# A state-space stage's time-step products at the first chunk, its decay mask on VectorE and its row gate on GpSimd

## The chip, the cores and the metric

The kernel runs on one core of one Trainium2 chip. The metric is the time of one execution on the device in microseconds (us), lower is better; where several runs are shown, their median counts.

## The reference, cut to what matters

The program is a whole eight-layer hybrid model over 8 sequences of 512 rows and 256 features. The change lies in the seventh layer alone, the state-space layer (512 inner features in 8 heads of 64, a state of 128):

```python
zxbcdt = u @ W_in
z, xBC, dt = split(zxbcdt)            # 512, 768 and 8 columns
dt = softplus(dt + dt_bias)
A = -exp(A_log)
xBC = silu(causal_conv_4(xBC, conv_w) + conv_b)
x, Bm, Cm = split(xBC)                # 512, 128, 128
y = ssd(x * dt, A * dt, Bm, Cm)       # decays exp(segsum), masked to the past
y = y.reshape(b, l, D_INNER)
y = (y - mu) * rsqrt(var + 1e-05) * norm_w
y = y * silu(z)
return y @ W_out
```

## The kernel before, in words

The stage is `state_space_stage`. It goes over the 8 sequences (the code calls each a batch, b) and cuts each into four chunks of 128 rows (c). Each engine has its own program, written out by hand and kept in step with the others by counting semaphores; nothing is reordered by a scheduler. The order of the work is the order of these four programs:

- `front` fills the pipeline with the projections of batch 0. Then `back(b, ...)` runs once per batch, and on TensorE it also carries the projections of batch b + 1 (`project`, 6 of them for the columns that are convolved and 4 for z), placed between the chunks of batch b. The last batch has none to carry.
- TensorE per chunk: `chunk_inputs` (L2196) transposes x, B and spreads the cumulative decays (`psX`, `psG`, `psC`), L2235 multiplies by the state, L2241 makes the state's update, and L2247 multiplies by the masked decays `lt` (result in `psY`).
- ScalarE turns `psC` into decays: `decays` (L2346) makes `lt` of 8 heads x 128 with Relu and Exp.
- GpSimd per chunk, in this order: `xdec` (L2414), which TensorE's L2241 needs; `st2` (L2418), which VectorE's state update needs; and the mask, `lt` times `gm` (L2422), which TensorE's L2247 needs.
- VectorE per chunk: `state` (L2514), `output` (L2522 adds up y; L2528 and L2530 take its statistics; L2532 is the gate, (y - mean) * silu(z)), `chunk_inputs(c + 2)` (L2496, L2501, L2502), `output_from_state` (L2507) and one `convolve` of the next batch (L2436, three operations).
- After the four chunks TensorE transposes the gated rows (L2255), multiplies them by the output weights (L2276, into the first 256 columns of `psG`), and VectorE adds the result to X (L2558). Between the first two transposes stands `project_dt` (L2154), the time-step products of batch b + 1: 24 products with 8 columns each, for the high and low halves of rows and weights, into `psO`. VectorE takes them with `dt_biased` (L2440) after the last chunk; `dt_decay`, `sum_dt` and `dt_sums` follow in the output part.

Of the kernel before, what the change touches and what calls it, by code (L numbers as in the profile page):

```python
# [2011 lines left out]
class StateSpaceWeights:  # L2012
# [3 lines left out]
    def __init__(self, core, w_in, conv_w, conv_b, dt_bias, a_log, norm_w, w_out, upto):  # L2016
# [3 lines left out]
        self.win_hi, self.win_lo = core.halves("sw_win_hi", [P, KD, WIN]), core.halves("sw_win_lo", [P, KD, WIN])  # L2020
        self.wout = sb("sw_wout", [P, KI, D])
# [7 lines left out]
        self.win_hi_done, self.win_done = core.sem("sw_win_hi_done"), core.sem("sw_win_done")  # L2029
        self.sources = (w_in, conv_w, conv_b, dt_bias, a_log, norm_w, w_out, upto)  # L2030
# [17 lines left out]
    def vector(self, nc, dve, b):  # L2048

        k = b - 3  # L2050
        if k in range(KD):
            dve.wait_ge(self.win_hi_done, k + 1)
            nc.vector.tensor_tensor(self.win_lo[:, k, :], self.win[:, k, :], self.win_hi[:, k, :],
                                    ALU.subtract).then_inc(self.win_done, 1)


def state_space_stage(nc, core, tag, sw):
# [5 lines left out]
    with ExitStack() as ctx:  # L2063
# [25 lines left out]
        psX = core.psum(f"{tag}_psX", [P, 512], ctx)  # L2089
        psG = core.psum(f"{tag}_psG", [P, 512], ctx)  # L2090
        psC = core.psum(f"{tag}_psC", [P, 2, 512], ctx)
# [12 lines left out]
            sem("yo_ps"), sem("yd_ps"), sem("st_ps"), sem("yo_done"), sem("y_done"), sem("st_done"), sem("st_step"))  # L2104
        ybn_done, ymv_done, yroot_done, yr_done, yz_done = (
# [13 lines left out]
        def _(pe):  # L2119
# [34 lines left out]
            def project_dt(b):  # L2154

                for j in range(TPB):
                    rows, out = slice(j * P, (j + 1) * P), psO[:, j * HM:(j + 1) * HM]
                    for k in range(KD):
                        dt_hi, dt_lo = win_hi[:, k, WIN - HM:WIN], win_lo[:, k, WIN - HM:WIN]
                        nc.tensor.matmul(out, x_hi[:, k, rows], dt_hi, start=(k == 0), stop=False)  # L2160
                        nc.tensor.matmul(out, x_hi[:, k, rows], dt_lo, start=False, stop=False)
                        last = nc.tensor.matmul(out, x_lo[:, k, rows], dt_hi, start=False, stop=(k == KD - 1))
                last.then_inc(dt_ps, 1)

            def sum_dt(b, v):

                steps = dv2[:, v, A].rearrange("p c h -> p (c h)")
                pe.wait_ge(dt_step, b * 7 + 4)
# [4 lines left out]
            def front():  # L2173
# [3 lines left out]
                pe.wait_ge(sw.win_done, KD)  # L2177
                for p in range(2):
# [8 lines left out]
            def back(b, u, more):  # L2187
# [6 lines left out]
                pe.wait_ge(dt_step, at(7, 7))  # L2194

                def chunk_inputs(c):  # L2196
# [25 lines left out]
                for c in range(TPB):  # L2222
# [13 lines left out]
                    if more and c:  # L2236
                        project(b + 1, 1 - u, 2 + c)
                    if c + 1 < TPB:
# [3 lines left out]
                                         start=True, stop=True).then_inc(st_ps, 1)  # L2242
                    pe.wait_ge(m_done, at(TPB, c + 1))
# [15 lines left out]
                if more:  # L2259
                    pe.wait_ge(yo_done, at(TPB - 1, TPB - 1))  # L2260
                    project_dt(b + 1)
                turn_gated(1)
                for j in range(TPB):
                    if j >= 2:
                        turn_gated(j)
                    if more:
                        project(b + 1, 1 - u, NCT + j)
                        if j == 2:
                            sum_dt(b + 1, 1 - u)
# [13 lines left out]
        def _(act):  # L2283
# [28 lines left out]
            def softplus(b, v):  # L2312

                dv = dv2[:, v]
                act.wait_ge(dt_step, b * 7 + 1)
# [22 lines left out]
            def back(b, u, more):  # L2338
# [4 lines left out]
                act.wait_ge(dt_step, at(7, 7))  # L2343
# [55 lines left out]
        def _(pool):  # L2399
# [4 lines left out]
            for b in range(B):  # L2404
                at = lambda per, c: b * per + c
                dv = dv2[:, b % 2]
                for c in range(TPB):
# [12 lines left out]
                    pool.wait_ge(lexp_done, at(TPB, c + 1))  # L2420
                    pool.wait_ge(g_done, at(TPB, c + 1))
                    tt(lt[:, c % 2], lt[:, c % 2], spread(gm[:, c % 2, :], [P, HM, P], 1), ALU.mult).then_inc(m_done, 1)  # L2422

        @block.vector
        def _(dve):
# [14 lines left out]
            def dt_biased(b, v):  # L2440
                dv = dv2[:, v]
                dve.wait_ge(dt_ps, b + 1)
                raw = psO[:, 0:TPB * HM].rearrange("p (c h) -> p c h", h=HM)
# [1182 lines left out]
```

## Time and profile before

| | before |
| --- | --- |
| median of 3 runs | 2611.42 us (2602.41 to 2615.07) |
| the profiled execution: its time, its span | 2603.77 us, 2601.8 us |
| mean granted TensorE clock | 0.957 of full speed |
| busy share of the span: PE, DVE, ACT, POOL | 86%, 68%, 54%, 44% |
| the state-space stage | 2091 to 2521 us of the span |
| first L2247 of a batch in the middle of the stage, and of the next | 2183.43, 2234.62 us |

PE is TensorE, DVE VectorE, ACT ScalarE, POOL GpSimd. The shares are means over stages with quite different limits, so the stage has to be read by itself. The granted clock is a share of full speed: 1.00 is 2.4 GHz, 0.50 is 1.2 GHz. The ends of matmuls are modelled, so neighbouring ones overlap in the rows, and starts are the safer figures.

### The profile page before, as it was taken

The numbers are of one execution on the slowest core, as the hardware profiler recorded it, in microseconds if no ns is written. First come the engines' busy times: TensorE is split into PE (matmuls) and PEld (weight loads), VectorE is DVE, ScalarE is ACT, GpSimd is POOL, SyncE is SP. The second block draws the span as 40 slices with busy tenths as digits, with TensorE's granted clock in tenths as the row PEclk, the third lists the DMA queues.
The fourth block names the chain that finished last, engine by engine and source line by source line (L and its number), as shares of the span: only waits on it lengthen the run. The fifth ranks groups of instructions, "written<-read, shape, count | busy, mean of one in ns | idle before, by whom it ended". The sixth has DMA issues, their size and how long they took to land. (4 is left out here: it accounts for less than half of the span.)

```text
span 2601.8 us, 56542 instructions
## 1 busy us (share of the span) xinstructions
PE 2230.6 (86%) x20944; PEld 1661.6 (64%) x20944; DVE 1773.7 (68%) x4400; ACT 1394.8 (54%) x2127; POOL 1155.8 (44%) x1181
## 2 busy tenths in 40 slices
PE   7957767777899898989899887999797979999979
PEld 4535555556797555555455455898566957777768
DVE  6666778777667667767767764896453558778753
ACT  4631222223342388878888885556111467777753
POOL 4438999992101267657656753000563012233220
PEclk9979999999899899999999999999999989999999
DMA  5454444551100111111111110000000000000001
GB/s 175 146 162 151 143 136 144 160 163 50 58 1 26 44 59 62 58 53 58 50 48 61 61 55 17 20 1 2 14 1 27 13 0 1 1 1 1 1 1 65
DMA packets 158739, 149.09 MB, mean 57 GB/s; under 512 B 21440, under 2 KB 141376, under 8 KB 155392
## 3 DMA queue, kind: packets, MB, share of 16 engines
q1 hardware_dynamic: 138704, 105.51, 13.5%
q0 software_dynamic: 3456, 23.07, 2.6%
q10 hardware_dynamic: 16304, 16.83, 2.2%
q8 instruction: 175, 2.87, 0.5%
q14 instruction: 100, 0.82, 0.1%
HBM read 100.51 MB, written 40.63 MB: 54 GB/s over the span
## 5 line engine op out<-in xcount | busy, mean ns | idle before, releaser
L1783 POOL TENSOR_SCALAR a_dist<-a_dist,a_mq 128x512 f32<-128x512 f32 x512 | 357.5, 720 | 122.2 <-ACT a_mq L1720 122.2
L1826 DVE TENSOR_SCALAR_CACHE_REDUCE a_dist<-a_ring 128x512 f32<-128x512 f32 x512 | 332.1, 687 | 91.8 <-PE a_ring L1469 90.3
L1710 ACT ACTIVATE a_pT<-a_psT 128x1024 f32<-128x1024 f32 x256 | 258.3, 1025 | 95.9 <-PE a_psT L1481 88.4
L1481 PE MATMUL a_psT<-ident,a_dist 128*128 128x128 f32 x2048 | 267.4, 278 | 18.0 <-ACT a_pT L1710 17.8
L1481 PEld LDWEIGHTS a_psT<-ident,a_dist 128*128 128x128 f32 x2048 | 236.5, 143 | 49.8 <-ACT a_pT L1710 19.9
L1704 ACT ACTIVATE a_dist<-a_dist 128x2048 f32<-128x2048 f32 x128 | 237.0, 1903 | 43.8 <-DVE a_dist L1826 40.8
L1469 PE MATMUL a_ring<-a_stack 102*128 102x512 bf16 x512 | 183.6, 396 | 57.1 <-DVE a_dist L1826 33.7
L1469 PEld LDWEIGHTS a_ring<-a_stack 102*128 102x128 bf16 x512 | 47.6, 98 | 228.7 <-DVE a_dist L1826 163.5
L3346 ACT ACTIVATE ds_wtm<-ds_wg,ds_par 128x256 f32<-128x256 f32 x64 | 29.2, 503 | 266.4 <-DVE ds_wg L3476 262.3
L1140 POOL TENSOR_TENSOR c_y<-c_prod 128x1024 f32<-128x1024 f32 x16 | 37.2, 2348 | 266.5 <-DVE c_prod L1174 264.9
L1494 PE MATMUL a_psO<-a_pT,a_va 128*32 128x512 f32 x1024 | 138.6, 618 | 2.3 <-ACT a_pT L1710 2.3
L2414 POOL TENSOR_TENSOR s_xdec<-s_xdt,s_dv 128x512 f32<-128x512 f32 x24 | 25.1, 1045 | 215.8 <-ACT s_dv L2345 206.0
L392 ACT ACTIVATE f_h<-a_psT,bf_bias_h 128x512 f32<-128x512 f32 x64 | 44.2, 690 | 130.3 <-PE a_psT L331 130.3
L2436 DVE SCALAR_TENSOR_TENSOR s_xbc<-s_padded,sw_cw,s_xbc 128x512 f32<-128x512 f32 x144 | 107.6, 749 | 4.2 <-ACT s_xbc L2304 0.6
L1761 POOL TENSOR_TENSOR bf_up<-a_raw 128x512 f32<-128x512 f32 x28 | 32.0, 1143 | 164.3 <-DVE a_raw L1838 164.3
L208 POOL TENSOR_TENSOR bf_t<-bf_up,bf_w 128x512 f32<-128x512 f32 x80 | 99.9, 1280 | 9.7 <-DMA bf_w<-in_up_w_dram 8.2
L2422 POOL TENSOR_TENSOR s_lt<-s_lt,s_gm 128x1024 f32<-128x1024 f32 x32 | 75.6, 2364 | 62.8 <-ACT s_lt L2355 62.8
L208 POOL TENSOR_TENSOR bf_t<-bf_down_t,bf_w 128x512 f32<-128x512 f32 x80 | 100.4, 1287 | 1.6
L1174 DVE TENSOR_TENSOR c_prod<-c_psF,lc_k 128x1024 f32<-128x1024 f32 x48 | 55.7, 1218 | 64.3 <-PE c_psF L1096 59.0
L435 DVE TENSOR_TENSOR f_h_lo<-f_h,f_h_hi 128x512 fp32r<-128x512 f32 x128 | 89.8, 702 | 4.4
L433 DVE CAST f_h_hi<-f_h 128x512 fp32r<-128x512 f32 x128 | 56.2, 439 | 40.0 <-ACT f_h L392 40.0
L392 ACT ACTIVATE f_h<-f_psH,bf_bias_h 128x512 f32<-128x512 f32 x64 | 44.2, 690 | 71.7 <-PE f_psH L331 71.7
(450 smaller groups left out, 6345.8 us busy)
## 6 DMA issues: line engine op xcount, KB each, us to landing
a_stack<-a_parts_dram SPq DMA_DIRECT2D x384, 64.0 KB
a_parts_dram<-a_parts SPq DMA_DIRECT2D x32, 384.0 KB, 2.5
bf_w<-in_up_w_dram POOLq DMA_DIRECT2D x10, 1024.0 KB, 8.1
bf_w<-in_down_w_dram POOLq DMA_DIRECT2D x10, 1024.0 KB, 7.3
ds_nbg<-tok_nbk ACTq DMA_DIRECT2D x128, 64.0 KB
feat_v<-di_part SPq DMA_DIRECT2D x16, 256.0 KB, 2.6
tok_nbk<-di_nbk SPq DMA_DIRECT2D x16, 256.0 KB, 3.0
feat_k<-di_part SPq DMA_DIRECT2D x16, 256.0 KB, 3.5
```

What stands on the lines that cost most here:

```text
L208: e.tensor_tensor(t, v[:, :, i % 2, :], w, ALU.mult).then_inc(self.step, 1)
L392: gelu = lambda out: nc.scalar.activation(out, psH[m % 2], ACT.Gelu, bias=self.bf.bias_h[:, m:m + 1])
L435: tt(self.h_lo[:, m, :], self.h[:, n % self.RING, :], self.h_hi[:, m, :], ALU.subtract).then_inc(self.h_lo_done, 1)
L1469: mm(to[:], stack[0:NROW, u, 0, i, q * P:(q + 1) * P], stack[0:NROW, u, 1, i, :], start=True, stop=True).then_inc(ring_in, 1)
L1481: last = turn(psT[:, u % 2, kb, q * P:(q + 1) * P], dist[:, g % 2, i, q, k * P:(k + 1) * P], core.ident[:])
L1494: last = mm(psO[i * PAD:(i + 1) * PAD, :], va[:, par, kb, c:c + PAD], pT[:, i, kb // 2, kb % 2, :], start=(kb == 0), stop=(kb == TPB - 1))
L1704: a(dist[:, g % 2, i], dist[:, g % 2, i], ACT.Sqrt)
L1710: a(pT[:, u // 2, u % 2], psT[:, u % 2], ACT.Exp).then_inc(exp_done, 1)
L1783: last = nc.gpsimd.tensor_scalar(d, d, -1.0, mq[:, g % 2, i, q:q + 1], ALU.mult, ALU.add)
L1826: ts(dist[:, gg % 2, i, q, :], ps[:], 1e-12, 3.0e38, ALU.max, ALU.min, accum_out=mq[:, gg % 2, i, q:q + 1]).then_inc(ring_out, 1)
L2422: tt(lt[:, c % 2], lt[:, c % 2], spread(gm[:, c % 2, :], [P, HM, P], 1), ALU.mult).then_inc(m_done, 1)
L2436: last = stt(o, src[:, j:j + S], cw[:, c, j:j + 1], o, ALU.mult, ALU.add)
```

## The change

Three things are done in the stage, and nothing outside it but two small operations that prepare a weight.

1. The time-step products. The high and low halves of their weights are laid side by side in a new tile `wdt`, made by VectorE in the mixture stage before. `project_dt` now has 16 products (8 with 16 columns, 8 with 8), writes to the free columns of `psG`, and stands in chunk 0, after L2262 (the state's update) and before the product with the decays. VectorE takes them in chunk 0 too, with one operation more, and TensorE's `chunk_inputs(2)` waits for that before it writes `psG` again. In chunk 3 the projection of the next batch goes ahead of the product with the state.
2. The mask, `lt` times `gm`, goes from GpSimd to VectorE (`masked`): once ahead of the chunks, then after `chunk_inputs(c + 2)`.
3. The gate goes from VectorE, where it is one operation, to GpSimd, where it is two: subtract the mean, multiply by silu(z).

```diff
+        self.wdt = core.halves("sw_wdt", [P, KD, 2, HM])
...
+        psDT = psG[:, D:D + 2 * TPB * HM]
...
                 for j in range(TPB):
-                    rows, out = slice(j * P, (j + 1) * P), psO[:, j * HM:(j + 1) * HM]
+                    rows = slice(j * P, (j + 1) * P)
+                    both, first = psDT[:, j * 2 * HM:(j + 1) * 2 * HM], psDT[:, j * 2 * HM:j * 2 * HM + HM]
                     for k in range(KD):
-                        dt_hi, dt_lo = win_hi[:, k, WIN - HM:WIN], win_lo[:, k, WIN - HM:WIN]
-                        nc.tensor.matmul(out, x_hi[:, k, rows], dt_hi, start=(k == 0), stop=False)
-                        nc.tensor.matmul(out, x_hi[:, k, rows], dt_lo, start=False, stop=False)
-                        last = nc.tensor.matmul(out, x_lo[:, k, rows], dt_hi, start=False, stop=(k == KD - 1))
+                        nc.tensor.matmul(both, x_hi[:, k, rows], sw.wdt[:, k].rearrange("p u h -> p (u h)"),
+                                         start=(k == 0), stop=(k == KD - 1), skip_group_check=True)
+                    for k in range(KD):
+                        last = nc.tensor.matmul(first, x_lo[:, k, rows], sw.wdt[:, k, 0, :], start=False,
+                                                stop=(k == KD - 1), skip_group_check=True)
...
                     if c:
                         pe.wait_ge(g_done, at(TPB, c))
+                        if more and c == 2:
+                            pe.wait_ge(dt_step, (b + 1) * 8 + 2)
...
+                    if more and c == TPB - 1:
+                        project(b + 1, 1 - u, 2 + c)
...
-                    if more and c:
+                    if more and 0 < c < TPB - 1:
                         project(b + 1, 1 - u, 2 + c)
...
+                    if more and c == 0:
+                        pe.wait_ge(g_done, at(TPB, 2))
+                        project_dt(b + 1)
                     pe.wait_ge(m_done, at(TPB, c + 1))
...
                 turn_gated(0)
-                if more:
-                    pe.wait_ge(yo_done, at(TPB - 1, TPB - 1))
-                    project_dt(b + 1)
                 turn_gated(1)
...
-                    pool.wait_ge(lexp_done, at(TPB, c + 1))
-                    pool.wait_ge(g_done, at(TPB, c + 1))
-                    tt(lt[:, c % 2], lt[:, c % 2], spread(gm[:, c % 2, :], [P, HM, P], 1), ALU.mult).then_inc(m_done, 1)
+                    pool.wait_ge(ymv_done, at(TPB, c + 1))
+                    nc.gpsimd.tensor_scalar(y[:, c, :], y[:, c, :], ymv[:, c, 0:1], None, ALU.subtract).then_inc(yc_done, 1)
+                    pool.wait_ge(yc_done, at(TPB, c + 1))
+                    tt(y[:, c, :], y[:, c, :], z2[:, b % 2, c, :], ALU.mult).then_inc(yz_done, 1)
...
-                    dve.wait_ge(ymv_done, at(TPB, c + 1))
-                    stt(y[:, c, :], y[:, c, :], ymv[:, c, 0:1], z2[:, u, c, :], ALU.subtract, ALU.mult).then_inc(yz_done, 1)
...
                 chunk_inputs(1)
+                masked(0)
                 for c in range(TPB):
                     if c + 1 < TPB:
                         state(c)
                     output(c)
+                    if more and c == 0:
+                        dt_biased(b + 1, 1 - u)
                     if c + 2 < TPB:
                         chunk_inputs(c + 2)
                     if c + 1 < TPB:
+                        masked(c + 1)
                         output_from_state(c + 1)
                         if more:
                             convolve(b + 1, 1 - u, c)
-                if more:
-                    dt_biased(b + 1, 1 - u)
```

How the order moves, first on VectorE in chunk 0 of a middle batch, before and after (`s_lt` are the decays, `s_gm` their mask, `s_xbc` the convolution's rows). Before:

```order
L2526 COPY s_y<-s_psY 128x512
L2528 BN_STATS s_ybn<-s_y 128x6
L2530 BN_AGGR s_ymv<-s_ybn 128x2
L2532 SCALAR_TENSOR_TENSOR s_y<-s_y,s_ymv,s_z 128x512
L2496 TENSOR_TENSOR s_xdt<-s_psX,s_dv 128x512
L2501 COPY s_b_tok<-s_psG 128x128
L2502 TENSOR_TENSOR s_gm<-s_psG,sw_tri 128x128
L2507 TENSOR_TENSOR s_yo<-s_psO,s_dv 128x512
L2436 SCALAR_TENSOR_TENSOR s_xbc<-s_padded,sw_cw,s_xbc 128x512 x3
```

And after:

```order
L2555 BN_AGGR s_ymv<-s_ybn 128x2
L2467 TENSOR_TENSOR s_dv<-s_psG,sw_dtb 128x32
L2469 TENSOR_TENSOR s_dv<-s_psG,s_dv 128x32
L2471 TENSOR_SCALAR s_dv<-s_dv 128x32
L2521 TENSOR_TENSOR s_xdt<-s_psX,s_dv 128x512
L2526 COPY s_b_tok<-s_psG 128x128
L2527 TENSOR_TENSOR s_gm<-s_psG,sw_tri 128x128
L2562 TENSOR_TENSOR s_lt<-s_lt,s_gm 128x1024
L2532 TENSOR_TENSOR s_yo<-s_psO,s_dv 128x512
L2459 SCALAR_TENSOR_TENSOR s_xbc<-s_padded,sw_cw,s_xbc 128x512 x3
```

The gate is gone from between the statistics and the chunk's inputs; the mask stands ahead of `s_yo` and the convolution, and in chunk 0 three small time-step operations come first.

GpSimd in a chunk in the middle of a batch, before:

```order
L2414 TENSOR_TENSOR s_xdec<-s_xdt,s_dv 128x512
L2418 TENSOR_TENSOR s_st<-s_st,s_dv 128x512
L2422 TENSOR_TENSOR s_lt<-s_lt,s_gm 128x1024
```

And after, with the first row of the next chunk:

```order
L2436 TENSOR_TENSOR s_xdec<-s_xdt,s_dv 128x512
L2440 TENSOR_TENSOR s_st<-s_st,s_dv 128x512
L2443 TENSOR_SCALAR s_y<-s_y,s_ymv 128x512
L2445 TENSOR_TENSOR s_y<-s_y,s_z 128x512
L2436 TENSOR_TENSOR s_xdec<-s_xdt,s_dv 128x512
```

`s_xdec` of a chunk stood behind the mask of the chunk before; it now stands behind that chunk's gate, which waits for the statistics of y.

## Rows read from the trace of the kernel before

**Rows 1.** Busy time of the engines over one batch; the column before the last two is PEclk.
```profile
2181.00:2235.00 54.00, 49.73 (x289) 40.68 (x288) 40.36 (x73) 41.26 (x88) 17.36 (x11) 0.97 0.00 1
```
**Rows 2.** Timeline of TensorE, one batch: start, duration (us), line, tiles, idle before.
```profile
2183.43 2.00 PE L2247 MATMUL s_psY<-s_xdt,s_lt 128*128 128x64 f32 x16 [1.17 <-POOL s_lt L2422]
...
2202.15 1.12 PE L2235 MATMUL s_psO<-s_st,s_xbc 128*128 128x512 f32 x2 [0.91 <-DVE s_st L2514]
...
2206.93 0.25 PE L2160 MATMUL s_psO<-sw_win_hi,s_x_hi 128*128 128x8 f32 x1
...
2209.50 0.25 PE L2162 MATMUL s_psO<-sw_win_hi,s_x_lo 128*128 128x8 f32 x1
...
2216.18 1.89 PE L2276 MATMUL s_psG<-sw_wout,s_yT 128*128 128x256 f32 x8
...
2232.42 1.02 PE L2241 MATMUL s_psX<-s_xdec,s_b_tok 128*128 128x512 f32 x2
2234.62 2.00 PE L2247 MATMUL s_psY<-s_xdt,s_lt 128*128 128x64 f32 x16 [1.18 <-POOL s_lt L2422]
```
**Rows 3.** Windows of one us, granted clock in the column before the last two.
```profile
2209.00:2210.00 1.00, 1.00 (x11) 1.00 (x11) 0.93 (x3) 0.92 (x2) 0.00 (x0) 1.00 0.06 16
2210.00:2211.00 1.00, 1.00 (x5) 0.86 (x4) 0.93 (x5) 0.57 (x2) 0.00 (x0) 0.50 0.00 0
2467.00:2468.00 1.00, 1.00 (x4) 0.81 (x3) 0.96 (x2) 0.98 (x2) 0.00 (x0) 0.50 0.00 0
```
**Rows 4.** Durations of one projection's products (ns, least/median/most).
```profile
L2150 PE MATMUL s_psP<-sw_win_lo,s_x_hi x64: 388/397/628, 2113.3 to 2479.2; 128*128 128x512 f32 x64
```
**Rows 5.** Timeline of VectorE, same batch.
```profile
2185.46 0.69 DVE L2526 COPY s_y<-s_psY 128x512 f32<-128x512 f32 x1 [2.48 <-PE s_psY L2247]
...
2193.59 0.68 DVE L2522 TENSOR_TENSOR s_y<-s_psY,s_yo 128x512 f32<-128x512 f32 x1
...
2195.25 2.42 DVE L2532 SCALAR_TENSOR_TENSOR s_y<-s_y,s_ymv,s_z 128x512 f32<-128x512 f32 x1
2197.59 0.68 DVE L2496 TENSOR_TENSOR s_xdt<-s_psX,s_dv 128x512 f32<-128x512 f32 x1
...
2198.58 0.68 DVE L2507 TENSOR_TENSOR s_yo<-s_psO,s_dv 128x512 f32<-128x512 f32 x1
...
2202.01 0.68 DVE L2522 TENSOR_TENSOR s_y<-s_psY,s_yo 128x512 f32<-128x512 f32 x1
...
2207.99 0.68 DVE L2522 TENSOR_TENSOR s_y<-s_psY,s_yo 128x512 f32<-128x512 f32 x1
```
**Rows 6.** Durations of the gate on VectorE (ns, least/median/most).
```profile
L2532 DVE SCALAR_TENSOR_TENSOR s_y<-s_y,s_ymv,s_z x32: 752/1560/2421, 2135.9 to 2509.1; 128x512 f32<-128x512 f32 x32
```
**Rows 7.** Timeline of GpSimd: the mask beside that gate.
```profile
2194.75 2.37 POOL L2422 TENSOR_TENSOR s_lt<-s_lt,s_gm 128x1024 f32<-128x1024 f32 x1
```
**Rows 8.** Timelines of the first stage, both engines with operands in SBUF.
```profile
75.27 1.48 POOL L2847 TENSOR_TENSOR di_sqr<-di_qk 128x512 f32<-128x512 f32 x1 [5.28 <-ACT di_qk L2793]
75.77 1.53 DVE L2913 TENSOR_TENSOR di_qk<-di_qk,di_ss 128x512 f32<-128x512 f32 x1
```
**Rows 9.** Groups by line and form, whole span, for prices (busy us, mean ns, idle before).
```profile
L968 DVE TENSOR_TENSOR ck_f<-ck_v,ck_f 128x1024 f32<-128x1024 f32 x1 | 1.2, 1215 | 0.0
L2444 DVE TENSOR_TENSOR s_dv<-s_psO,sw_dtb 128x32 f32<-128x32 f32 x8 | 1.5, 186 | 5.5 <-PE s_psO L2162 5.5
L1783 POOL TENSOR_SCALAR a_dist<-a_dist,a_mq 128x512 f32<-128x512 f32 x512 | 357.5, 720 | 122.2 <-ACT a_mq L1720 122.2
L216 POOL TENSOR_TENSOR bf_up<-bf_t 128x512 f32<-128x512 f32 x40 | 50.2, 1277 | 1.6
L2414 POOL TENSOR_TENSOR s_xdec<-s_xdt,s_dv 128x512 f32<-128x512 f32 x24 | 25.1, 1045 | 215.8 <-ACT s_dv L2345 206.0 <-DVE s_xdt L2496 9.8
```
**Rows 10.** Timeline of TensorE, last batch: products of chunks 0 and 3.
```profile
2489.37 2.00 PE L2247 MATMUL s_psY<-s_xdt,s_lt 128*128 128x64 f32 x16 [1.56 <-POOL s_lt L2422]
...
2505.19 2.00 PE L2247 MATMUL s_psY<-s_xdt,s_lt 128*128 128x64 f32 x16
```

More of the change, by code:

```diff
@@ L2054, in vector @@
                                     ALU.subtract).then_inc(self.win_done, 1)
+        if b == B - 3:
+            steps = self.win[:, :, 2 * DI + 2 * NST:]
+            nc.vector.tensor_copy(self.wdt[:, :, 0, :], steps).then_inc(self.wdt_hi_done, 1)
+            dve.wait_ge(self.wdt_hi_done, 1)
+            nc.vector.tensor_tensor(self.wdt[:, :, 1, :], steps, self.wdt[:, :, 0, :],
+                                    ALU.subtract).then_inc(self.wdt_done, 1)
 def state_space_stage(nc, core, tag, sw):
@@ L2177, in front @@
                 pe.wait_ge(sw.win_done, KD)
+                pe.wait_ge(sw.wdt_done, 1)
                 for p in range(2):
@@ L2193, in back @@
                 pe.wait_ge(silu_done, at(NCT, NCT))
-                pe.wait_ge(dt_step, at(7, 7))
+                pe.wait_ge(dt_step, at(8, 8))
                 def chunk_inputs(c):
@@ L2208, in chunk_inputs @@
                         pe.wait_ge(g_done, at(TPB, c))
+                        if more and c == 2:
+                            pe.wait_ge(dt_step, (b + 1) * 8 + 2)
                     elif b:
                         pe.wait_ge(x_done, at(TPB, 0))
+                    else:
+                        pe.wait_ge(dt_step, 2)
                     nc.tensor.transpose(psG[:, 0:NST], xbc[:, KI, q], core.ident[:])
@@ L2268, in back @@
                         if j == 2:
+                            pe.wait_ge(yo_done, at(TPB - 1, TPB - 1))
                             sum_dt(b + 1, 1 - u)
@@ L2314, in softplus @@
                 dv = dv2[:, v]
-                act.wait_ge(dt_step, b * 7 + 1)
+                act.wait_ge(dt_step, b * 8 + 2)
                 a(dv[:, AB], dv[:, XD], ACT.Abs).then_inc(dt_act, 1)
@@ L2342, in back @@
                     take_rows(b + 1)
-                act.wait_ge(dt_step, at(7, 7))
+                act.wait_ge(dt_step, at(8, 8))
                 for o, i in ((EOUT, CS), (DEC, DIF), (ETOT, TOT)):
@@ L2442, in dt_biased @@
                 dve.wait_ge(dt_ps, b + 1)
-                raw = psO[:, 0:TPB * HM].rearrange("p (c h) -> p c h", h=HM)
-                tt(dv[:, XD], raw, spread(dtb[:], [P, TPB, HM], 1), ALU.add).then_inc(dt_step, 1)
-                dve.wait_ge(dt_step, b * 7 + 1)
+                raw = psDT.rearrange("p (c u h) -> p c u h", u=2, h=HM)
+                tt(dv[:, XD], raw[:, :, 0, :], spread(dtb[:], [P, TPB, HM], 1), ALU.add).then_inc(dt_step, 1)
+                dve.wait_ge(dt_step, b * 8 + 1)
+                tt(dv[:, XD], raw[:, :, 1, :], dv[:, XD], ALU.add).then_inc(dt_step, 1)
+                dve.wait_ge(dt_step, b * 8 + 2)
                 ts(dv[:, RL], dv[:, XD], 0.0, None, ALU.max).then_inc(dt_step, 1)
@@ L2449, in dt_decay @@
                 dv = dv2[:, v]
-                dve.wait_ge(dt_step, b * 7 + 2)
+                dve.wait_ge(dt_step, b * 8 + 3)
                 dve.wait_ge(dt_act, b * 6 + 3)
@@ L2530, in output, with masked @@
                     nc.vector.bn_aggr(ymv[:, c, :], ybn[:, c, :]).then_inc(ymv_done, 1)
-                    dve.wait_ge(ymv_done, at(TPB, c + 1))
-                    stt(y[:, c, :], y[:, c, :], ymv[:, c, 0:1], z2[:, u, c, :], ALU.subtract, ALU.mult).then_inc(yz_done, 1)
                 if more:
                     rest_of_rows(b + 1)
+                def masked(c):
+                    dve.wait_ge(lexp_done, at(TPB, c + 1))
+                    dve.wait_ge(g_done, at(TPB, c + 1))
+                    tt(lt[:, c % 2], lt[:, c % 2], spread(gm[:, c % 2, :], [P, HM, P], 1), ALU.mult).then_inc(m_done, 1)
                 chunk_inputs(0)
                 chunk_inputs(1)
+                masked(0)
                 for c in range(TPB):
```

8 lines of the change are left out of this document (5 added, 3 removed).

## The prediction

> **What bounds the kernel now.** I read the busy times by batch first. In the stage TensorE is busy 49.7 of 54 us, VectorE 40.4, ScalarE 41.3, GpSimd 17.4 [rows 1]. So TensorE sets the pace, with little room: VectorE needs only a few us more per batch to take over. Next its timeline. From the first product with the decays of one batch to that of the next it takes 2234.62 - 2183.43 = 51.19 us [rows 2], seven times in all. Two waits of that stretch matter here: for GpSimd's mask ahead of that product (1.18 us in the row; 1.3 if TensorE is free 0.9 after 2232.42, an estimate) and for the state (0.91). Others are of half a us. The time-step products run from 2206.93 to 2209.50 [rows 2], 24 at a distance of 0.111, 2.67 us for almost no columns.
>
> Then the clock. TensorE is busy all the time up to 2210, and at 2210 the granted clock is 0.50, 1.2 GHz; a later batch shows the same at 2467 [rows 3]. It comes once per batch, straight behind the time-step products. A projection's product takes up to 628 ns there against a median of 397 [rows 4], and six of them run so: about 1.4 us lost per batch.
>
> Last the timeline of VectorE, since its chain is the one that the change lengthens. From one addition of y to the next it takes 8.13, 8.42 and 5.98 us (2185.46, 2193.59, 2202.01, 2207.99) [rows 5]. TensorE waits 0.91 at 2202.15 for the state that VectorE makes [rows 2]: in the later chunks VectorE already leads.
>
> **A lock between VectorE and GpSimd.** The gate takes 0.75 us alone and up to 2.42 [rows 6]. The long one starts at 2195.25 and ends at 2197.67; GpSimd's mask runs from 2194.75 to 2197.12 [rows 5, 7]. Subtract 0.75 and the gate starts 0.2 before the mask's recorded end: it stood until the mask let go. In the first stage it goes both ways: a GpSimd operation of 1.05 takes 1.48, then VectorE's of 0.68 takes 1.53 [rows 8], as if each waits for the other's current operation and they alternate. A GpSimd operation of 1.05 thus holds VectorE for about 0.9. All these VectorE operations read two tensors from SBUF, as do the mask and the convolution. The Trainium skill (SBUF — State Buffer, Who interferes with whom) says this against the change: a Vector instruction with two SBUF inputs and a GpSimd instruction that reads SBUF exclude each other, and whichever issues second is blocked until the first has finished. By that rule a hold would be the full 1.05, 0.15 more than the rows show, some 0.5 us more per batch.
>
> **The change, part by part, for one of the seven middle stretches.**
>
> Time-step products: 16 instead of 24 at 0.111 is 1.78 us, 0.89 less work. They now start where TensorE waited for the mask, at about 2233.3, and end at 2235.1: the product with the decays comes 0.45 later than at 2234.62. In return 2.67 us and the slow clock's 1.4 leave the output part. Both count only if TensorE leads there.
>
> The mask on VectorE: 1.21 us for 1024 elements with both inputs in SBUF [rows 9], 1.13 as a step of a row of operations. On GpSimd it is 2.37.
>
> The gate on GpSimd: subtraction 0.70 (0.72 in the row [rows 9]), multiplication of two full tensors 1.28 by the butterfly's row, 1.05 by `xdec`'s, which has one broadcast operand. I take 1.28, as its operands are like the butterfly's, and keep 1.05 as the lower end. With 0.06 between them VectorE is locked out until 1.9 us behind the statistics.
>
> What that makes of VectorE's chain:
> - chunk 0 to 1: 8.13, less the gate's 2.0, plus three small operations 0.6 (0.19 each [rows 9]), plus mask 1.1. It comes to the mask 1.6 behind the statistics (0.6 and the inputs' 1.0: 2197.59 to 2198.58 [rows 5]) and waits 0.3. `xdec` and `st2` now queue behind the gate, and so meet the convolution: one hold of 0.9 and the rest of another, 1.0 in all. Sum 9.1, +1.0.
> - chunk 1 to 2: 8.42 - 2.34 + 1.13, plus 0.9 for the gate, plus 1.0 at the convolution: 9.1, +0.7.
> - chunk 2 to 3: 5.98 - 1.5 (the gate's median less the overlap) + 1.13 + 1.0, the gate's multiplication inside the convolution: 6.6, +0.6.
> - from there to the second output product: 2216.18 - 2207.99 = 8.19 [rows 2, 5]. TensorE would be there 4 us sooner, but this product must wait for the first addition to X. That is sums and statistics 1.7, root and reciprocal 0.6, convolution 2.25, 1.0 for the lock, X 0.5: 6.0, so -2.2.
>
> Sum +0.1, and +0.45 at the end of the stretch: 51.7, **+0.55** per batch. The gains are real but stand in front of a late VectorE. The wait of `chunk_inputs(2)` for the time-step operations (0.5) lies in these chunks, where TensorE waits for the state anyhow.
>
> The last batch has no projections to cover anything. From chunk 0 to chunk 3 it takes 2505.19 - 2489.37 = 15.8 [rows 10]. Now: product 1.9, sums and statistics 1.7, gate 1.9, mask 1.0, `xdec` 1.1, update 0.9: 8.5 to chunk 1, 8.5 to chunk 2, and 4.9 to chunk 3, whose mask has to wait for VectorE's statistics where GpSimd was free before. 21.9, +6.1. Its first product comes 1.1 sooner, the mask being 1.2 shorter.
>
> The fill: eight small products less, -0.9. The two operations for `wdt` lie in a stage where VectorE is busy about 60% of the time: nothing; if they are not hidden, 0.4.
>
> Together: 6 x 0.55 = 3.3, the seventh stretch, behind which no products are made, 0.1 - 1.1 = -1.0, +6.1, -0.9: 7.5, say **+8 us**. The profiled execution's 2603.77 becomes about 2612. The median of the runs shown is 7.6 above that execution, so the median becomes about **2619**.
>
> **Rivals.**
> 1. *The lock does not bite.* If mask and convolution run beside the gate, the 4.9 us of holds per batch go and TensorE leads again: about 47.7 per stretch, -3.5, seven times, and +4 in the last batch: 20 us faster, 2591. For: `convolve` shows no stretched row today, though `xdec` runs close by. Against: rows 5 to 8. A milder form, the gate at 1.05 and short holds, gives +2. Chance of faster by over 13 us: 14%.
> 2. *The clock falls all the same.* The new products (1.8 us) stand directly ahead of those with the decays (1.75), which have 64 columns each: 3.5 us with few columns, and a wait, product, transposes and wait at chunk 3. The clock would fall in chunk 1, where TensorE and VectorE are almost level, and 1 to 1.5 us per batch come back: 7 to 11 us more, 2627. Above +13 us this is slower. The Trainium skill (TensorE: Matmul & The Clock Gate, HAM oscillation) blames gaps in which TensorE is idle; by the rows it fell while TensorE was busy at every moment, so removing waits need not prevent it. Chance 25%.
> 3. *Every convolution operation loses the lock once.* GpSimd has four operations per chunk where it had three; if each stops one of VectorE's for 0.9, a full chunk costs 1.5 more than I put in: 4 per batch, +28, 2650. It decides as soon as GpSimd's queue runs dry later than VectorE's convolution begins. Chance 8%.
> In chunk 0 `xdec` has no gate ahead of it, so that the products miss the wait they should fill is hardly to be feared.
>
> **How the numbers follow.** The forecast, 53%, holds +2 (gate at 1.05) to +12 (holds of 1.05 by the whole operation, weight preparation not hidden). About 0.5%, 13 us, is what a measurement can tell from no change; the runs shown span 12.7. Slower: all of rivals 2 and 3, 33%, and 1% from the forecast's upper end: 34%. Faster: rival 1, 14%. Same: what is left, 52%. The range reaches from most of rival 1 over the upper end of rival 2, with 6 to 8 us for the spread of the runs: 2597 to 2637; rival 3 and the far half of rival 1 are left out.
>
> **What would show it.** In the profile after: the stretch between first products near 51.7; the clock at 1.00 behind the first transposes; masks on VectorE of 1.21 for chunks 0 and 3 but 2 us for chunk 2; one convolution operation per chunk near 1.5 instead of 0.75; a wait of TensorE for VectorE's X of over 1 us ahead of the second output product; the last batch's chunks 8.5 apart. I am wrong if VectorE's masks and convolutions keep their bare durations, or if the clock still falls in every batch.

## The result, and the profile after

The changed kernel takes 2637.4 us (median of 8 runs, 2623.9 to 2646.4), the kernel before 2609.6 us in runs on the same chip. The ratio is 1.0105, 95% interval 1.0080 to 1.0129: slower by 1%, where +8 us was forecast and +28 came, just past the upper end of the forecast's range (2637). The profiled execution has a span of 2632.1 us against 2601.8.

The stretches give the loss more sharply than the spans. VectorE's copy of chunk 0's product stands once in each batch; the first and the last of the eight bound the seven stretches, before and after:

```profile
2134.26 0.69 DVE L2526 COPY s_y<-s_psY 128x512 f32<-128x512 f32 x1 [2.48 <-PE s_psY L2247]
2491.40 0.69 DVE L2526 COPY s_y<-s_psY 128x512 f32<-128x512 f32 x1 [2.87 <-PE s_psY L2247]
```
```profile
2132.70 0.69 DVE L2551 COPY s_y<-s_psY 128x512 f32<-128x512 f32 x1 [2.76 <-PE s_psY L2271]
2511.98 0.69 DVE L2551 COPY s_y<-s_psY 128x512 f32<-128x512 f32 x1 [1.49 <-PE s_psY L2271]
```

Seven stretches took 357.1 us and take 379.3: +22.1, or 3.2 per batch (forecast 0.55). The last batch runs from 2509.95 to 2534.13, 24.2 us where it was 15.8 [rows 10] (forecast 21.9):

```profile
2509.95 2.00 PE L2271 MATMUL s_psY<-s_xdt,s_lt 128*128 128x64 f32 x16 [0.40 <-DVE s_lt L2562]
...
2534.13 2.03 PE L2271 MATMUL s_psY<-s_xdt,s_lt 128*128 128x64 f32 x16 [1.94 <-DVE s_lt L2562]
```

22.1 and 8.4 less 1.5 for the sooner start are 29 of the 30 us of the span. Over the same window as [rows 1] TensorE is busy 48.75 instead of 49.73 and VectorE 42.4 instead of 40.4. VectorE has 2 us more to do and TensorE 1 us less, and it was TensorE that set the pace: it waits more.

```profile
2181.00:2235.00 54.00, 48.75 (x272) 39.71 (x271) 42.41 (x71) 37.95 (x80) 20.17 (x14) 0.94 0.00 1
```

For what it waits is in its list of waits over the eight batches (total us, times, longest). Before, the top of that list was 9.8 us for GpSimd's mask; `xdec` did not stand in it:

```profile
PE s_psX L2262 <- POOL s_xdec L2436: 24.9, 13, 3.5
PE s_psG L2298 <- DVE X L2588: 10.6, 8, 1.7
```

GpSimd's timeline in one batch shows why `xdec` is late. The statistics end at 2352.6; the gate holds GpSimd for four microseconds, and `xdec` and `st2` stand behind it:

```profile
2352.68 1.56 POOL L2443 TENSOR_SCALAR s_y<-s_y,s_ymv 128x512 f32<-128x512 f32 x1 [8.63 <-DVE s_ymv L2555]
2354.32 2.35 POOL L2445 TENSOR_TENSOR s_y<-s_y,s_z 128x512 f32<-128x512 f32 x1
2356.64 1.48 POOL L2436 TENSOR_TENSOR s_xdec<-s_xdt,s_dv 128x512 f32<-128x512 f32 x1
2358.08 1.49 POOL L2440 TENSOR_TENSOR s_st<-s_st,s_dv 128x512 f32<-128x512 f32 x1
```

TensorE, same batch. It waits 1.50 and 2.54 us for `xdec`, and the product with the decays behind the second wait runs at half clock, 3.25 us instead of 1.89:

```profile
2353.02 0.30 PE L2230 MATMUL s_psG<-ident,s_xbc 128*128 128x128 f32 x1 [0.25 <-DVE s_dv L2469]
...
2358.17 1.13 PE L2262 MATMUL s_psX<-s_xdec,s_b_tok 128*128 128x512 f32 x2 [1.50 <-POOL s_xdec L2436]
2359.14 1.89 PE L2271 MATMUL s_psY<-s_xdt,s_lt 128*128 128x64 f32 x16
...
2367.47 1.12 PE L2262 MATMUL s_psX<-s_xdec,s_b_tok 128*128 128x512 f32 x2 [2.54 <-POOL s_xdec L2436]
2368.44 3.25 PE L2271 MATMUL s_psY<-s_xdt,s_lt 128*128 128x64 f32 x16
```

The granted clock (column before the last two) is 0.50 in two places inside the chunks now, behind chunk 0's product with the decays (2189) and behind that of chunk 2 (2371, 2427). Before, it was so in the eight batches only in the output part [rows 3]; there it is 1.00 now:

```profile
2189.00:2190.00 1.00, 1.00 (x4) 0.77 (x3) 0.93 (x4) 0.00 (x0) 0.00 (x0) 0.50 0.00 0
...
2371.00:2372.00 1.00, 1.00 (x5) 0.93 (x5) 0.27 (x1) 0.00 (x0) 0.00 (x0) 0.50 0.00 0
2427.00:2428.00 1.00, 1.00 (x4) 0.81 (x4) 0.76 (x2) 0.00 (x0) 0.00 (x0) 0.50 0.00 0
```

Last the durations (ns, least/median/most) of what was moved, and of what shares the lock with it:

```profile
L2443 POOL TENSOR_SCALAR s_y<-s_y,s_ymv x32: 1558/1564/2456, 2134.4 to 2537.9; 128x512 f32<-128x512 f32 x32
L2445 POOL TENSOR_TENSOR s_y<-s_y,s_z x32: 1264/1522/2347, 2136.1 to 2539.6; 128x512 f32<-128x512 f32 x32
L2562 DVE TENSOR_TENSOR s_lt<-s_lt,s_gm x32: 1203/1215/1829, 2128.1 to 2532.9; 128x1024 f32<-128x1024 f32 x32
L2436 POOL TENSOR_TENSOR s_xdec<-s_xdt,s_dv x24: 1037/1484/2028, 2124.7 to 2527.3; 128x512 f32<-128x512 f32 x24
```

The subtraction never takes less than 1.56 us, where 0.70 was put in. VectorE's mask mostly keeps its bare 1.21; GpSimd loses the lock more often, its `xdec` rising from 1.05 [rows 9] to 1.48.

### The profile page after: what moved, and what is told of

It reads as the page before. It is cut to its first block and busy times, and to the rows that moved or that the text cites. A ratio compares the mean times of both kernels' runs of the same rounds, so it can differ in the third digit from the quotient of the medians.

```text
span 2632.1 us, 56470 instructions
## 1 busy us (share of the span) xinstructions
PE 2238.2 (85%) x20880; PEld 1669.2 (63%) x20880; DVE 1797.1 (68%) x4410; ACT 1392.6 (53%) x2127; POOL 1198.9 (46%) x1213
## 5 line engine op out<-in xcount | busy, mean ns | idle before, releaser
L2459 DVE SCALAR_TENSOR_TENSOR s_xbc<-s_padded,sw_cw,s_xbc 128x512 f32<-128x512 f32 x144 | 139.7, 972 | 4.2 <-ACT s_xbc L2326 0.5
L2443 POOL TENSOR_SCALAR s_y<-s_y,s_ymv 128x512 f32<-128x512 f32 x32 | 57.1, 1786 | 155.6 <-DVE s_ymv L2555 155.6
L2436 POOL TENSOR_TENSOR s_xdec<-s_xdt,s_dv 128x512 f32<-128x512 f32 x24 | 33.9, 1414 | 133.5 <-ACT s_dv L2367 133.5
L2271 PEld LDWEIGHTS s_psY<-s_xdt,s_lt 128*128 128x128 f32 x512 | 71.2, 218 | 19.5 <-DVE s_lt L2562 9.8
```

The lines of the kernel that those rows point to most:

```text
L2271: last = nc.tensor.matmul(psY[:, h * PM:(h + 1) * PM], lt[:, c % 2, h, :], xdt[:, c % 2, h * PM:(h + 1) * PM], start=True, stop=True)
L2443: nc.gpsimd.tensor_scalar(y[:, c, :], y[:, c, :], ymv[:, c, 0:1], None, ALU.subtract).then_inc(yc_done, 1)
L2459: last = stt(o, src[:, j:j + S], cw[:, c, j:j + 1], o, ALU.mult, ALU.add)
```

## The experiments

Three theories, which the recorded expectations name by letter. **A**: the gate on GpSimd is the cost, by its size, its place in the queue, or the lock. **B**: the slow clock is, and the new place of the time-step products brings it down. **C**: the mask on VectorE is. "Seven stretches" is always the time between the first and the last of the eight copies in the profiled execution; how early an execution reached the stage varies by over 20 us, so I compare these beside the medians. A step is the time from one chunk's product with the decays to the next chunk's. "Output part" is from chunk 3's product to the next batch's first.

| run | median us | ratio to before, 95% | seven stretches | last batch |
| --- | --- | --- | --- | --- |
| before | 2605.7 to 2609.6 | | 357.1 | 15.8 |
| changed | 2637.4 | 1.0080 to 1.0129 | 379.3 | 24.2 |
| e1 gate on VectorE | 2622.7 | 1.0033 to 1.0073 | 365.4 | 19.7 |
| e2 steps alone | 2616.8 | 1.0017 to 1.0052 | 370.9 | 15.8 |
| e3 mask alone | 2620.8 | 1.0037 to 1.0079 | 366.7 | 19.6 |
| e4 gate form | 2616.0 | 1.0009 to 1.0052 | 358.1 | 23.1 |
| e5 xdec first | 2603.9 | 0.9967 to 0.9999 | 355.7 | 16.6 |
| e6 steps back | 2640.5 | 1.0077 to 1.0160 | 372.2 | 24.7 |
| e8 form, xdec first | 2605.6 | 0.9974 to 1.0002 | 355.8 | 19.0 |
| e9 steps taken early | 2590.2 | 0.9915 to 0.9962 | 345.8 | 16.2 |
| e11 and mask on VectorE | 2613.2 | 1.0015 to 1.0055 | 359.7 | 21.4 |
| e13 projection between | 2587.1 | 0.9900 to 0.9957 | 343.2 | 15.8 |
| e15 xdec first, taken early | 2591.2 | 0.9930 to 0.9969 | 348.4 | 16.6 |
| e17 all repaired | 2602.6 | 0.9977 to 1.0013 | 354.2 | 16.6 |

**e1, the gate back on VectorE.**

```diff
-                    nc.gpsimd.tensor_scalar(y[:, c, :], y[:, c, :], ymv[:, c, 0:1], None, ALU.subtract).then_inc(yc_done, 1)
...
+                    stt(y[:, c, :], y[:, c, :], ymv[:, c, 0:1], z2[:, u, c, :], ALU.subtract, ALU.mult).then_inc(yz_done, 1)
```

> The changed kernel with the gate back on VectorE as one operation; time-step products and mask stay where the change puts them. Theory A (the gate on GpSimd is the cost: 1.56 + 1.3 us instead of 0.75, with xdec and st2 queued behind it): the stretch from batch to batch falls from 54.8 to 50 to 51.5, the last batch from 24.2 to 16 to 17, in all 2600 to 2612. Theory B (the clock, which the time-step products ahead of the sparse product with the decays bring down in chunk 0 and again in chunk 1): the clock still falls twice per batch, the stretch stays above 53, 2625 or more. Theory C (the mask on VectorE makes its chain the bound): 2625 or more, with TensorE waiting for masks.

15 us of 28 go, so the gate's place is about half of it; neither A's 2600 to 2612 nor the others' 2625 came. The rest does not: TensorE waits 20.5 us for VectorE's masks (longest 2.7, ahead of chunk 3's product), and 5.3 for the time-step operations.

**e2, the time-step products alone** (mask on GpSimd, gate on VectorE).

> The kernel before with the time-step products alone moved and packed; mask on GpSimd and gate on VectorE as before. Theory A: 1.3 us less per batch in the output part and nothing back in chunk 0, where TensorE waits for the mask anyhow: stretch 50 to 51, 2600 to 2607. Theory B: the clock falls behind the product with the decays of chunk 0 and in chunk 1, stretch 53 or more, 2620 or more. Theory C: as A.

I expected a gain by theory A and it costs 10 us. Theory B named stretches of 53 or more, and they are 53.0 in the mean, with the clock falling in the first step of all seven batches; its 2620 didn't come. In six batches of seven that step, 8.03 us before, is 11.9. The rows say why: TensorE's transposes of chunk 2 wait 2.04 us for VectorE's operations, these for the gate, and the gate (1.73 instead of 0.75) for GpSimd's mask. Behind the wait the clock is at half: the next spread of decays takes 1.91 instead of 1.04.

```profile
2181.62 0.30 PE L2230 MATMUL s_psG<-ident,s_xbc 128*128 128x128 f32 x1 [2.04 <-DVE s_dv L2468]
...
2181.99 1.91 PE L2236 MATMUL s_psC<-ident,s_dv 128*128 128x128 f32 x8
```
```profile
2179.42 1.73 DVE L2556 SCALAR_TENSOR_TENSOR s_y<-s_y,s_ymv,s_z 128x512 f32<-128x512 f32 x1
2181.07 0.18 DVE L2466 TENSOR_TENSOR s_dv<-s_psG,sw_dtb 128x32 f32<-128x32 f32 x1
```

**e3, the mask alone.**

> The kernel before with the mask alone moved to VectorE; gate on VectorE, time-step products at their old place. Theory A: VectorE takes over 3.4 us of masks per batch and loses up to 3 us of waiting for the lock, TensorE's waits for masks become shorter or longer by less than 1 us: 2608 to 2618, last batch 16. Theory B: as A. Theory C: VectorE becomes the bound, stretch 53 or more, 2625 or more.

Between A and C. The step from chunk 2 to 3 is 6.55 us instead of 5.38, since VectorE now makes the mask of chunk 3 behind chunk 2's statistics and gate; the last batch takes 3.8 more for the same reason; and the output part is 29.6 to 32.9 in the first six batches, where it was 29.9.

**e4, the subtraction in another form.** The mean's sign is turned, and put right in the output weights.

```diff
-                    nc.gpsimd.tensor_scalar(y[:, c, :], y[:, c, :], ymv[:, c, 0:1], None, ALU.subtract)
+                    nc.gpsimd.tensor_scalar(y[:, c, :], y[:, c, :], -1.0, ymv[:, c, 0:1], ALU.mult, ALU.add)
```

> The changed kernel with the gate's subtraction on GpSimd written as y times -1 plus the mean (multiply, add), the sign put right in the output weights; all else as changed. Theory A, in the form that the subtraction's size of 1.56 us comes from its operation and not from its operands: it takes 0.72 as the same form does in another stage, every chunk gets 0.84 us of GpSimd back, stretch 53 to 54, last batch 21 to 22, 2620 to 2628. If the size comes from the operands or from GpSimd losing the lock: 1.56 and 2637 as before. Theory B: the subtraction may shrink, but the clock still falls twice per batch and the time stays above 2630.

The operation falls to what the prediction had put in, and with it the kernel to what it had forecast: +9 us, the first six stretches 51.4 to 52.0 (forecast 51.7), last batch 23.1. That is better than this run's own expectation (2620 to 2628, stretch 53 to 54).

```profile
L2443 POOL TENSOR_SCALAR s_y<-s_y,s_ymv x32: 692/692/1581, 2134.8 to 2517.5; 128x512 f32<-128x512 f32 x32
```

The prediction's sum can be read here term by term. From one addition of y on VectorE to the next, and from the last to TensorE's second output product, five batches of seven take 9.07, 9.07, 6.39 and 5.99 us; the terms were 9.1, 9.1, 6.6 and 6.0:

```profile
2339.64 0.69 DVE L2551 COPY s_y<-s_psY 128x512 f32<-128x512 f32 x1 [2.77 <-PE s_psY L2271]
...
2348.71 0.68 DVE L2547 TENSOR_TENSOR s_y<-s_psY,s_yo 128x512 f32<-128x512 f32 x1
...
2357.78 0.68 DVE L2547 TENSOR_TENSOR s_y<-s_psY,s_yo 128x512 f32<-128x512 f32 x1
...
2364.17 0.69 DVE L2547 TENSOR_TENSOR s_y<-s_psY,s_yo 128x512 f32<-128x512 f32 x1
```
```profile
2370.16 1.97 PE L2298 MATMUL s_psG<-sw_wout,s_yT 128*128 128x256 f32 x8 [1.22 <-DVE X L2588]
```

VectorE has no idle row between these four, so its chain does set the pace there. The clock still fell in the first step of two of the seven batches (9.6 us instead of 8.8, the stretch 0.4 to 0.6 longer) and in the last batch, but never over chunk 2's product. So most of the changed kernel's slow clock followed from the long gate. Of its seven stretches, five have chunk 2's product partly or wholly at half clock; the other two are 52.5 and, the seventh, 49.8, where e4 has 51.4 and 48.7. An estimate from these: the gate's size costs 1.1 us a stretch by itself, 8 in all, and the slow clock behind chunk 2's wait the other 14 of the 22.

**e14, what makes the subtraction slow** (one execution, 2599.5 us, order of e5). Chunk 3's rows are gated by y + mean there.

> What the subtraction of 1.56 us owes its size to. The order of the run with xdec first; the first operation of the gate is written in another form in each chunk: chunk 0 subtracts with no second operation (as the change does), chunk 1 subtracts and multiplies by 1.0, chunk 2 multiplies by 1.0 and subtracts, chunk 3 adds the mean with no second operation (so the rows of chunk 3 are gated by y + mean, which the reference does not do). If the size comes from the missing second operation: chunks 0 and 3 take 1.56, 1 and 2 0.69. If it comes from subtract: 0, 1 and 2 take 1.56, chunk 3 0.69. If it comes from the per-partition mean as the first scalar: 0, 1 and 3 take 1.56, chunk 2 0.69.

None of the three. The rows of chunks 0 to 3 of one batch: subtract alone 1.57, subtract then multiply 2.01, multiply then subtract 2.88, add alone 1.57.

```profile
2338.05 1.57 POOL L2448 TENSOR_SCALAR s_y<-s_y,s_ymv 128x512 f32<-128x512 f32 x1 [2.70 <-DVE s_ymv L2560]
2347.08 2.01 POOL L2448 TENSOR_SCALAR s_y<-s_y,s_ymv 128x512 f32<-128x512 f32 x1 [0.52 <-DVE s_ymv L2560]
2354.82 2.89 POOL L2448 TENSOR_SCALAR s_y<-s_y,s_ymv 128x512 f32<-128x512 f32 x1 [4.38 <-DVE s_ymv L2560]
2361.25 1.57 POOL L2448 TENSOR_SCALAR s_y<-s_y,s_ymv 128x512 f32<-128x512 f32 x1 [2.20 <-DVE s_ymv L2560]
```

In all eight batches the four read so within 0.02 us. Some of the 2.01 and 2.88 may be lock. Multiply-and-add at 0.69 (e4) is the exception; each of these four forms takes at least twice as long. That single form was the one that I had taken the price from.

**e5, GpSimd's order.**

```diff
+                prepare(0)
                 for c in range(TPB):
+                    if c + 1 < TPB - 1:
+                        prepare(c + 1)
                     pool.wait_ge(ymv_done, at(TPB, c + 1))
```

Here `prepare` holds `xdec` and `st2`, as they were.

> The changed kernel (subtraction of 1.56 us kept) with GpSimd's order changed: xdec and st2 of the next chunk go ahead of the gate of this one. Theory A1 (the gate costs because xdec and st2 queue behind it): TensorE's wait for xdec, 24.9 us in the changed kernel, goes, stretch 51 to 52.5 against 54.8, last batch 21, 2610 to 2620. Theory A2 (the gate costs because it holds VectorE by the lock wherever it stands): the waits for xdec turn into waits for VectorE's state and masks, stretch 54 or more, 2630 or more.

A1, and more than it promised: 33 us less than the changed kernel, with the subtraction still at 1.56. The wait for `xdec` is gone from the list, `xdec` is back at its bare duration, and the last batch takes 16.6. The clock stays at 1.00 inside the chunks, but it is 0.50 again in every output part, for 6.8 us each, and that part is back at 29.8 us (28.4 to 28.9 in the changed kernel).

```profile
L2433 POOL TENSOR_TENSOR s_xdec<-s_xdt,s_dv x24: 1041/1045/1498, 2122.5 to 2491.0; 128x512 f32<-128x512 f32 x24
```

**e8, both repairs of the gate.**

> The changed kernel with both repairs of the gate: the subtraction as multiply-add (0.69 us), and xdec and st2 of the next chunk ahead of it on GpSimd. Theory A1: TensorE's wait for xdec (17.1 us in the run with the form alone) goes, chunks of 8 to 8.5 instead of 8.8 to 9.1, stretch 49.5 to 50.5 against 51.5, last batch 19 to 21; 2598 to 2608, the first version level with or faster than the kernel before. Theory A2: stretch as in the run with the form alone, 2614 to 2618.

Level with before and with e5, and the stretch is 51.2, not the 49.5 to 50.5 expected: once nobody queues behind the gate, its length is worth nothing. The two repairs do not add up; they take away the same wait. In the last batch the shorter gate even costs 2.4 us: `xdec` starts sooner, beside VectorE's mask, and takes 2.02 (2490.30) where e5 has 1.04 (2490.97), and the clock is at half for 3.4 us there, in e5 not at all.

**e6, the time-step products back** (mask and gate as changed).

> The changed kernel without its first part: 24 time-step products behind the first gated transposes and taken by VectorE at the end, as before; mask on VectorE and gate on GpSimd (1.56 us) as changed. Theory B (the time-step products in chunk 0 bring the clock down there): 5 us or more less in all than the changed kernel's chunks, the clock no longer falls in chunk 1; the output part grows by 1 to 2 us per batch; stretch 53 to 54, 2620 to 2632. Theory A (the gate alone): the chunks keep their 10 us each, stretch 54.5 to 56.5, 2635 to 2645.

The median is A's, 3 us above the changed kernel's with intervals that overlap. The first step stays at 9.8, TensorE waits 33.8 us for `xdec`, and the clock still falls inside the chunks of the first three batches and of the last, with no small product there. In the other four stretches of this execution it doesn't, and three of them measure 51.2 and the seventh 49.8. So the small products aren't needed for the fall over chunk 2's product. The fall in the first step is another matter: five batches of seven have it in the changed kernel and none here. The same step in the same batch, changed kernel and e6 (granted clock 0.83 and 1.00 in the mean):

```profile
2186.00:2196.00 10.00, 10.00 (x51) 7.79 (x51) 6.66 (x13) 6.85 (x19) 5.86 (x4) 0.83 0.01 2
```
```profile
2190.00:2200.00 10.00, 8.31 (x48) 6.40 (x48) 8.13 (x13) 9.55 (x25) 5.63 (x4) 1.00 0.00 0
```

The traces of all runs agree. In the three kernels without small products in chunk 0 (before, e3, e6) the clock falls in this step in no batch of 21. In those that have them it falls in seven batches of seven (e2), five (changed), four (e15), three (e11), two (e1, e4, e9) or one (e8, e13, e14, e17), and in e5 in none. They are needed for this fall and do not bring it on each time. In the changed kernel it shows no cost (the step takes 9.7 to 10.3 with it and 10.2 without); in e9 it does, below.

**e9, the time-step products taken early.**

```diff
+                    if more and c == 0:
+                        dt_biased(b + 1, 1 - u)
                     output(c)
-                    if more and c == 0:
-                        dt_biased(b + 1, 1 - u)
```

On top of e2.

> The run with the time-step products alone (mask on GpSimd, gate on VectorE), with VectorE's three small operations on them put ahead of chunk 0's output, where VectorE waits 2 us for TensorE, instead of behind the gate. If the 2.04 us for which TensorE's transposes of chunk 2 wait for these operations is what made that run slower: the wait goes, the first step of a batch falls from 11.9 to 8.5 to 10, stretch 50 to 51.5, 2600 to 2608. If the slow clock behind the small products made it slower: the clock still falls in chunk 1 of most batches, the step stays above 10.5 and the time at 2612 or more.

The wait of 2.04 goes, the step is 8.0 in five batches, and the kernel is faster than before by 18 us, more than the 2600 to 2608 expected; e2 was slower by 10. In the other two batches the clock falls in that step, which takes 9.6; the stretch of the first of them is 49.9 instead of 48.6. VectorE does the three operations while it waits for TensorE anyhow:

```profile
2328.95 0.19 DVE L2466 TENSOR_TENSOR s_dv<-s_psG,sw_dtb 128x32 f32<-128x32 f32 x1 [0.99 <-PE s_psG L2175]
2329.18 0.19 DVE L2468 TENSOR_TENSOR s_dv<-s_psG,s_dv 128x32 f32<-128x32 f32 x1
2329.41 0.99 DVE L2470 TENSOR_SCALAR s_dv<-s_dv 128x32 f32<-128x32 f32 x1
2330.79 0.69 DVE L2550 COPY s_y<-s_psY 128x512 f32<-128x512 f32 x1 [0.39 <-PE s_psY L2271]
```

The output part is 27.7 us in most batches, 29.8 in two. The difference is the clock again: in the first batch it is at half from 2154 to 2160 and a projection's product takes 0.63, in the second it is not and they take 0.40, behind the same row of work (a wait of 1.17, the product with the decays, four transposes, a wait of 0.78).

```profile
2155.24 1.09 PE L2279 MATMUL s_psX<-ident,s_y 128*128 128x128 f32 x4 [0.78 <-ACT s_yT L2397]
...
2158.26 0.63 PE L2163 MATMUL s_psP<-sw_win_hi,s_x_lo 128*128 128x512 f32 x1
```
```profile
2205.76 0.63 PE L2279 MATMUL s_psX<-ident,s_y 128*128 128x128 f32 x4 [0.78 <-ACT s_yT L2397]
...
2207.39 0.39 PE L2163 MATMUL s_psP<-sw_win_hi,s_x_lo 128*128 128x512 f32 x1
```

**e15, the whole change with e5's order and e9's place.**

> The whole change, with xdec and st2 ahead of the gate on GpSimd (subtraction of 1.56 us kept) and with VectorE's operations on the time-step products put ahead of chunk 0's output. If what is left over of the change against the best split (2590) is the wait for those operations (0.2 us) and 0.6 us of VectorE's chain: stretch 50 to 50.7, 2595 to 2600. If it is the slow clock over the product with the decays of chunk 3 and the output part (29.8 instead of 27.7 us in every batch): the first step gets 0.5 shorter at most and the clock stays, 2600 to 2605.

12.8 us less than e5 (medians of two sets of runs, in which before took 2608.6 and 2608.0), more than the 0.8 us per batch named: the output part goes from 29.8 to 28.45 in all batches but the first, and the clock no longer falls there. In the first step it now falls in four batches (9.6 us against 8.0). The whole change can gain, then, but mask and gate add nothing to e9.

**e11, e9 plus the mask on VectorE.**

> The time-step products taken early and the mask on VectorE, the gate on VectorE too: the run with the steps taken early plus the mask's move alone. If the mask's move costs what it did by itself (VectorE's chain, 6.55 us instead of 5.4 from chunk 2 to chunk 3, last batch 19.6 instead of 15.8): 12 to 14 us over 2590, so 2600 to 2604. If the mask's cost was only the wait and the clock in the output part: 2588 to 2594.

23 us over e9, more than either case said. TensorE waits 20.5 us for VectorE's masks, as in e1, and in five of the seven output parts the clock is at half for 6.8 us or more (e9: two). The mask on VectorE is a loss as long as the gate stays there.

**e13, a projection between the first transposes** (on e9), and **e17**, the same on e15.

```diff
                 turn_gated(0)
+                if more:
+                    project(b + 1, 1 - u, NCT)
                 turn_gated(1)
```

The loop behind then leaves this projection out.

> The run with the steps taken early, and in the output part the first z projection moved between the first two gated transposes, where TensorE waits 0.78 us for ScalarE's copy of the first. If that wait costs its own length: 0.8 us less per batch, 5 us in all. If the clock's fall there (2153 and the like, in two batches of seven, 2.1 us each) hangs on the row of wait, product with the decays, transposes, wait, then the fall goes too: 7 to 10 us less, 2580 to 2585, the output part near 26.9 in every batch. If the projection only moves and TensorE then waits for X or ScalarE instead: 2588 to 2592.

> The whole change with xdec and st2 ahead of the gate, the time-step products taken early, and the first z projection between the first two gated transposes. If the slow clock and the waits between these transposes are the rest: output part 27 to 28 in every batch, stretch 49 to 49.5, 2582 to 2588, below the run without the projection's move (2591). If TensorE then waits for VectorE's first X (8.0 us of such waits already): 2588 to 2593, nothing gained.

e13 measures 2587.1 against e9's 2590.2, intervals that overlap: neither the expected gain of 5 to 10 us nor clearly none. In its trace no output part is above 28.5, so the long fall of the clock (6.8 us, in two batches of e9) is absent there, but TensorE now waits 7.0 us for X instead of 2.2: the wait of 0.78 was only handed on. In e17 it is worse: the second output product waits 2.16 us for VectorE's X and then runs at half clock, 3.40 us instead of the 1.97 of e15. The output part is 30.1 where e15 has 28.45, and e17 is slower than e15 by 11 us, where 2582 to 2593 had been expected. Its profiled execution is the slowest of its 13; it reached the stage 22 us later than e15's, so I read the stage's rows and not the span.

```profile
PE s_psG L2301 <- DVE X L2593: 14.2, 8, 2.2
```
```profile
2382.02 3.40 PE L2301 MATMUL s_psG<-sw_wout,s_yT 128*128 128x256 f32 x8 [2.16 <-DVE X L2593]
```

Why X itself comes so late there I didn't follow further.

## Why the prediction was wrong

- **The failed step** is the gate on GpSimd, "subtraction 0.70 (0.72 in the row)". It measured 1.56, since the row was a multiply-and-add and the change subtracts (e4, e14). With the form of the row the stretch is 51.6 in the mean of six (forecast 51.7), the last batch 23.1 (21.9), the whole +9 (+8), and the four terms of VectorE's chain come out within about 0.2 each. So the mechanism of the sum was right, and that +9 is not luck of terms that cancel; only the last batch was put 1.2 too low.
- **What the size was multiplied by** was not in the sum. I let `xdec` and `st2` "queue behind the gate" and charged only VectorE's holds for it, 1.0 per chunk. Who waits for `xdec` is TensorE: 24.9 us in the changed kernel, and behind the wait of chunk 2 its clock falls. Length and queue cost only together: in this order the shorter subtraction is worth 21 us (e4), without the queue nothing (e8), and the order alone is worth 33 (e5).
- **Rival 2**, the clock falling in chunk 1, is two falls. The one that it describes, behind small products and the product with the decays of chunk 0, came in five batches of seven and only in kernels with these products there; its price of 1 to 1.5 us shows in e9 (1.3) and not in the changed kernel. The dear one, over chunk 2's product, no rival named: it comes without small products too (e6), follows a wait of TensorE for `xdec` (2.1 to 2.6 us in every batch of both kernels, with the fall in five and in three), and is gone with a shorter gate (e4, the wait 1.6) or another order (e5). It costs 1.3 us at the product itself and more behind it: the step from chunk 2 to 3 is 7.0 to 7.3 us in four batches where it is 4.75 in the two at full clock. The sum had put the clock at nothing inside the chunks. "The slow clock's 1.4 leave the output part" held in the changed kernel: the first projection behind the first transposes runs at 0.40 (2379.52 and on). It didn't hold in e5 and e8, whose output parts are slow in all batches and in all but one.
- **Rival 3**, each convolution operation held once: in chunk 1 the three together took 4.05 to 4.07 us in every batch, against 2.33 bare. That is 1.7, where I had 1.0 and the rival 2.5. In chunks 0 and 2 it is mostly 0.8 and 0.9, near the 1.0 put in. Rival 1 did not come: the lock bites.
- **The time-step products**: their -0.9 in the fill can't be read, since starts vary by over 20 us between executions. "A wait of 0.5 in chunks where TensorE waits for the state anyhow" held with the gate on GpSimd (0.25 in the changed kernel) and only so: with the gate still ahead of the operations it was 2.04 (e2), and e9 shows 26 us for the place of three operations of 0.19, slow clock behind the wait included.
- **The mask**: priced right (1.21). I expected it to be locked out behind the gate for 0.3 and 0.9. With the short gate of e4 it was (1.49 and 2.31 for the masks of chunks 1 and 2); in the changed kernel it mostly won the lock, and GpSimd waited.
- **The wait for the first X** of over 1 us ahead of the second output product came: 10.6 us in eight.

## What to carry to other kernels

Take the price of an operation from a row of the same engine with the same operation, not only the same shape: here one form of a tensor-scalar operation on GpSimd took 0.69 us and four others 1.57 to 2.88. When work is moved to an engine, list what stands behind it in that queue and who waits for that; ordering the queue by what the bottleneck engine needs was worth 33 us here, and once that was done, a subtraction of less than half the length was worth nothing. A new wait of the bottleneck engine may cost more than its length: 14 of the 22 us here were the slow clock behind it. And look for an engine's own waiting time before placing small operations: the same three operations cost 26 us more behind the gate than ahead of the output.

## What the runs showed of the hardware

- GpSimd's tensor-scalar operation of 512 elements by form: multiply-add 0.69 (e4), add or subtract alone 1.57, subtract-multiply 2.01, multiply-subtract 2.88 (e14; some of the last two may be lock).
- The lock binds GpSimd as much as VectorE: in the changed kernel a multiplication of 1.26 took up to 2.35, `xdec` of 1.04 up to 2.03. It also binds a VectorE operation with one SBUF input: the clamp of 128x32 (L2470 in e9) took 0.18 alone, 0.48 in the changed kernel and 0.99 in e9, where it began beside GpSimd's `st2` and ended with it (2330.36 and 2330.40). The Trainium skill (SBUF — State Buffer, Who interferes with whom) says that a tensor-scalar operation can enter a mode that takes the shared port. The trace agrees that the clamp is held, 0.99 against 0.18; which mode it was in, it doesn't show.
- The granted clock falls or not behind rows of work that look alike: in e9's output part in two batches of seven, in its first step in two others. It fell with TensorE busy at every moment behind small products (before, at 2210), and over a product behind a wait of 2.54 without them nearby (changed, 2368.44). What tips it stays open.
